# A two-stage conv block with a selective scan: C times B in wide GpSimd products ahead of the decays

## What is computed

```
x = x + _L0_conv_ref(_gn(x), ...)    # 8 experts: one scale for each image and channel
x = x + _L1_conv_ref(_gn(x), ...)    # selective scan, below

# _L1_conv_ref, N = 1024 tokens, 2 heads of 128 channels, S = 8 states
xz = silu(in_proj_w @ x + in_proj_b);  x_ssm, res, gate = split(xz, 3)
xf = silu(depthwise_conv3(x_ssm, dw_w) + dw_b)      # along the tokens
dbc = dbc_w @ xf + dbc_b                            # for each head 1 + 2*S rows: dt, B, C
dt = softplus(dt);  A = -exp(A_log)
# tokens in the order perm[head] (argsort of a Mobius map of the grid)
h_t = exp(dt_t * A) * h_(t-1) + dt_t * B_t * x_t    # for each state
y_t = sum over states of C_t * h_t,  + D[head] * x_t
# back to the image's order
y = y * silu(gate) + res
out = silu(out_proj_w @ y + out_proj_b)
```

## Time and profile before

| | |
|---|---|
| median of 3 runs | 1252.72 us (1245.59 to 1258.89) |
| span of the profiled execution | 1174.1 us; the profile does not give that execution's time as a run |
| PE busy | 961.5 us, 82% of the span |
| DVE, ScalarE, GpSimd busy | 588.0, 579.1, 532.4 us |
| stretch 543 to 674 us (phase 3): PE, DVE, ScalarE, GpSimd busy | 116.2, 64.2, 66.9, 68.5 of 131 us |
| chain that ended last | PE 41%, DMA 21%, GpSimd 16%, issue 10%, DVE 5%, SP's queue 4%, ScalarE 3% |
| GpSimd's `weigh` (L413) | 256 instructions, 182.1 us |
| DVE's product, reduction, diagonal and `mblk` (L1038, L1040, L1043, L1049) | 16 each, 38.8 + 59.4 + 7.8 + 36.7 us |
| ScalarE's table loads for softplus (L532, L534) | 8 each, 1283 ns one |

### The profile page before, as it was taken

The page is one execution under the profiler, slowest core; times in us unless marked ns, Lnnn a source line. Parts: engine busy times, 40 slices in busy tenths (PEclk is TensorE's granted clock), DMA queues, the critical chain, the costliest instruction groups (busy, mean ns, idle before and its releaser), DMA issues.

```text
span 1174.1 us, 12950 instructions
## 1 busy us (share of the span) xinstructions
PE 961.5 (82%) x3988; PEld 597.9 (51%) x3988; DVE 588.0 (50%) x1104; ACT 579.1 (49%) x1078; POOL 532.4 (45%) x628
## 2 busy tenths in 40 slices
PE   1039666997899988998899779997999889978966
PEld 0035445664467445754476346744575357634643
DVE  5966136534572448444753348243853466345613
ACT  4824423345734564547444564456553754456341
POOL 0002527164555627371826545471936373644340
PEclk9558765798899998999899989998999899998987
DMA  8830290135912391247513491238313661348122
GB/s 331 331 120 1 81 157 1 36 119 155 216 36 93 101 226 71 72 133 183 140 37 121 144 213 48 78 101 192 121 63 122 179 162 37 119 152 148 37 94 86
DMA packets 112051, 142.54 MB, mean 121 GB/s; under 512 B 41705, under 2 KB 91122, under 8 KB 111986
## 3 DMA queue, kind: packets, MB, share of 16 engines
q1 hardware_dynamic: 99698, 105.91, 34.0%
q0 software_dynamic: 12288, 35.80, 9.4%
HBM read 88.07 MB, written 53.61 MB: 121 GB/s over the span
## 4 chain that ended last, share of the span: by engine, by line
PE 41%; DMA 21%; POOL 16%; issue 10%; DVE 5%; SPq 4%; ACT 3%; POOLq 0%; ACTq 0%; DVEq 0%
PE pj L1183 12%; POOL xt_scratch L389 10%; PE pj L1258 9%; PE pj L1256 8%; DMA xb<-in_x 7%; DMA cd_scratch<-xp 6%; POOL big L401 4%; SPq L302 4%; PE st L1230 3%; DMA xp<-xt_scratch 2%; DMA xt_scratch<-stage,idx 2%; PE tp L1241 2%; PE tp L1206 2%; DMA crow<-cd_scratch 2%; POOL big L413 2%
## 5 line engine op out<-in xcount | busy, mean ns | idle before, releaser
L1183 PE MATMUL pj<-xb,wsc 128*128 128x512 f32 x768 | 392.1, 658 | 39.0 <-DMA xb<-in_x 26.6
L413 POOL TENSOR_TENSOR big<-big,crow 128x128 f32<-128x128 f32 x256 | 182.1, 751 | 212.6 <-DMA crow<-cd_scratch 199.1
L1183 PEld LDWEIGHTS pj<-xb,wsc 128*128 128x128 f32 x768 | 155.0, 213 | 205.9 <-issue 197.7
L389 POOL DMA_INDIRECT xt_scratch<-stage,idx x128 | 139.6, 1091 | 83.0 <-DVE stage L941 46.4
L358 POOL TENSOR_SCALAR wsc<-inw,pcur 128x256 f32<-128x256 f32 x96 | 62.6, 669 | 239.1 <-PE pj L1183 150.7
L401 POOL DMA_INDIRECT big<-yt_scratch,idx x128 | 130.5, 1020 | 75.5 <-issue 37.7
L1258 PE MATMUL pj<-ch 64*128 64x128 f32 x512 | 129.2, 333 | 0.0
L1256 PE MATMUL pj<-xp,mblk 128*128 128x128 f32 x512 | 120.1, 318 | 4.2 <-ACT xs L519 4.2
L1304 PE MATMUL pj<-gt,outw 128*128 128x512 f32 x256 | 111.8, 594 | 0.1
L995 DVE TENSOR_TENSOR_SCAN hs<-big,st 128x64 f32<-128x64 f32 x256 | 49.0, 265 | 101.8 <-PE st L1230 101.8
L570 ACT COPY ch<-tp 128x256 f32<-128x256 f32 x128 | 45.4, 376 | 106.6 <-PE tp L1242 106.6
(11 more groups left out here) (192 smaller groups left out, 1348.7 us busy)
## 6 DMA issues: line engine op xcount, KB each, us to landing
xb<-in_x SPq DMA_DIRECT2D x32, 1024.0 KB, 7.4
xp<-xt_scratch SPq DMA_DIRECT2D x8, 2048.0 KB, 10.0
crow<-cd_scratch SPq DMA_DIRECT2D x128, 128.0 KB, 7.8
yt_scratch<-rs SPq DMA_DIRECT2D x16, 1024.0 KB, 4.4
out<-xb SPq DMA_DIRECT2D x16, 1024.0 KB, 10.2
xp<-xt_scratch SPq DMA_DIRECT2D x8, 272.0 KB, 3.5
xt_scratch<-stage,idx POOLq DMA_INDIRECT x128
big<-yt_scratch,idx POOLq DMA_INDIRECT x128, 2.7
```

The costliest lines, as they stand in the source:

```text
L389: pool.indirect_dma_start(out=xt_d.ap(), out_offset=bass.IndirectOffsetOnAxis(ap=idx[:, k:k + 1], axis=0), in_=v(stage, (nt * H + h) * ROW ...
L413: last = nc.gpsimd.tensor_tensor(v(big, W_OFF + (s * Q + b * NT) * L, (L, NT), (1, L)), v(big, s * EEW + SEG + b * NT * L, (L, NT), (1, L) ...
L1183: last = nc.tensor.matmul(o[:, :], v(wsc, (b * CT + ct) * 2 * C + slot * C + ot * P, (1, P)), x_view(par, b, ct, nt * HALF, HALF), start=( ...
```

## The change

- **Products.** `weigh(i, h)` on GpSimd becomes `products(i, h)`. In place of decays times C, in 16 instructions of 128 columns, it forms C times (dt * B), in two instructions of 1024 columns, one for each image, and then adds the diagonal D (`dskip`) to state 0's part, 256 columns. It waits for `crow`, for `bc_step` (dt * B) and for the area at `W_OFF` to be free, and no longer for the decays.
- **DVE.** `token_weights` multiplies this by the decays, in one product of 2048 columns, and sums the eight states by three additions of 1024, 512 and 256 columns. The strided reduction (L1040) and the diagonal (L1043) go. `mblk` is written in two instructions, one for each image, and PE's `result` waits for its own image's.
- **Decays.** `decays(i, 1)` waits for DVE's product (`m_step`), since that is now what reads head 0's decays.
- **Table.** ScalarE's `softplus` starts with the load of the one table set that has both exp and ln.
- **`dskip`**, D on the diagonal for each head, is made once by two small DVE instructions ahead of `take_params(0, 0)`.

```diff
--- before.py
+++ after.py
@@ -122,8 +122,10 @@
         prm = sb("prm", B * PRM_W)
         pcur = sb("pcur", 2 * NB * PRM_W)
         idx = sb("idx", H * NT, U32)
+        dskip = sb("dskip", H * L)
         W_OFF = S * EEW
         A_SUM, A_SQ = 400, 400 + B
+        DB, DBE, CS = 0, Q * S, 2 * Q * S
 
 
         INB, DWW, DWB, OUTB, DBCB, ANEG, DPAR, MOB = 0, 6, 12, 14, 16, 50, 66, 68
@@ -178,6 +180,7 @@
         sg_full = sem("sg_full")
         ee_ready = sem("ee_ready")
         w_ready = sem("w_ready")
+        w_step = sem("w_step")
         bc_step = sem("bc_step")
         bblk_ready = sem("bblk_ready")
         cblk_ready = sem("cblk_ready")
@@ -394,7 +397,7 @@
                 hold(y_stored[h], 16 * (i + 1))
                 if h == 0:
 
-                    hold(mblk_ready, H * (i + 1))
+                    hold(mblk_ready, H * NB * (i + 1))
                     hold(hs_ready, H * NB * S * (i + 1))
                 for nt in range(NT):
                     k = h * NT + nt
@@ -402,19 +405,24 @@
                         out=v(big, k * NB * P, (1, NB * P)), out_offset=None, in_=yt_d.ap()[0:(h + 1) * N],
                         in_offset=bass.IndirectOffsetOnAxis(ap=idx[:, k:k + 1], axis=0)).then_inc(y_gathered[h], 16)
 
-            def weigh(i, h):
-
-                hold(ee_ready, i * H + h + 1)
+            def products(i, h):
+
                 hold(crow_in[h], 16 * CPT * (i + 1))
 
-                hold(m_step, (i * H + h) * 3)
-                for s in range(S):
-                    for b in range(NB):
-                        last = nc.gpsimd.tensor_tensor(
-                            v(big, W_OFF + (s * Q + b * NT) * L, (L, NT), (1, L)),
-                            v(big, s * EEW + SEG + b * NT * L, (L, NT), (1, L)),
-                            v(crow, h * NT * L * S * NB + s * NB + b, (L * S * NB, NT), (S * NB, L)), ALU.mult)
-                last.then_inc(w_ready, 1)
+                hold(bc_step, (i * H + h) * 3 + 1)
+
+                hold(m_step, (i * H + h) * 4)
+                if h == 0:
+
+                    hold(y_full, i * Y_U)
+                for b in range(NB):
+                    nc.gpsimd.tensor_tensor(
+                        v(big, W_OFF + b * NT * L, (Q * L, S), (1, NT * L)),
+                        v(crow, h * NT * L * S * NB + b, (NB, S), (S * NB, NT * L)),
+                        v(bc8, DB + b * NT * S, (1, S), (S, NT), (0, L)), ALU.mult).then_inc(w_step, 1)
+                hold(w_step, (i * H + h + 1) * NB)
+                skip = v(big, W_OFF, (L, Q), (1, L))
+                nc.gpsimd.tensor_tensor(skip, skip, v(dskip, h * L, (0, Q), (1, L)), ALU.add).then_inc(w_ready, 1)
 
             def first_tap(i, b):
 
@@ -427,14 +435,14 @@
 
             def cycle(i, par, half):
                 more = not last_phase(i)
-                weigh(i, 0)
+                products(i, 0)
                 if more:
                     if not first(i):
                         hold(pcur_ready, i + 2)
                         weights_x(i + 1, 1 - par, 0)
                     weights_x(i + 1, 1 - par, 1)
                 weights_residual(i, par)
-                weigh(i, 1)
+                products(i, 1)
                 if more:
                     weights_gate(i + 1, 1 - par, 0)
                     weights_gate(i + 1, 1 - par, 1)
@@ -528,6 +536,7 @@
 
             def softplus(i):
 
+                nc.scalar.preload_act_table_set("natural_log_exp_and_others")
                 act.wait_ge(sp_v, i * 9 + 1)
                 nc.scalar.activation(v(dts, 32, (1, 32)), v(dts, 0, (1, 32)), ACT.Exp, scale=-1.0).then_inc(sp_a, 1)
                 act.wait_ge(sp_v, i * 9 + 2)
@@ -541,7 +550,7 @@
                     wait(act, y_full, i * Y_U)
                 else:
 
-                    act.wait_ge(w_ready, i * H + h)
+                    act.wait_ge(m_step, (i * H + h - 1) * 4 + 1)
                     act.wait_ge(hs_ready, (i * H + h) * NB * S)
                 for s in range(S):
                     last = nc.scalar.activation(v(big, s * EEW, (1, EEW)), v(sg, 0, (1, EEW)), ACT.Exp,
@@ -942,7 +951,6 @@
 
             HQ = H * Q
             AXO, UO, WO, LO, MO, DO = 0, 32, 64, 96, 128, 192
-            DB, DBE, CS = 0, Q * S, 2 * Q * S
 
             def part(h, off):
                 return h * NT * ROW + NB * P + off
@@ -1034,20 +1042,23 @@
 
                 ih = i * H + h
                 dve.wait_ge(w_ready, ih + 1)
-                W = v(big, W_OFF, (Q * L, S), (L, Q), (1, L))
-                nc.vector.tensor_tensor(W, W, v(bc8, DB, (1, S), (S, Q), (0, L)), ALU.mult).then_inc(m_step, 1)
-                dve.wait_ge(m_step, ih * 3 + 1)
-                nc.vector.tensor_reduce(m16[:, :], v(big, W_OFF, (1, Q * L), (Q * L, S)), AX.X, ALU.add).then_inc(m_step, 1)
-                dve.wait_ge(m_step, ih * 3 + 2)
-
-                nc.vector.scalar_tensor_tensor(v(m16, 0, (L, Q), (1, L)), const("diag", (0, Q), (1, L)),
-                                               v(small, DPAR + h, (1, 1)), v(m16, 0, (L, Q), (1, L)),
-                                               ALU.mult, ALU.add).then_inc(m_step, 1)
-                dve.wait_ge(m_step, ih * 3 + 3)
+                dve.wait_ge(ee_ready, ih + 1)
+                states = lambda s0, n: v(big, W_OFF + s0 * Q * L, (Q * L, n), (1, Q * L))
+                nc.vector.tensor_tensor(states(0, S), v(big, SEG, (EEW, S), (1, Q * L)), states(0, S), ALU.mult).then_inc(m_step, 1)
+                dve.wait_ge(m_step, ih * 4 + 1)
+                nc.vector.tensor_tensor(states(0, 4), states(0, 4), states(4, 4), ALU.add).then_inc(m_step, 1)
+                dve.wait_ge(m_step, ih * 4 + 2)
+                nc.vector.tensor_tensor(states(0, 2), states(0, 2), states(2, 2), ALU.add).then_inc(m_step, 1)
+                dve.wait_ge(m_step, ih * 4 + 3)
+                nc.vector.tensor_tensor(m16[:, :], v(big, W_OFF, (1, Q * L)), v(big, W_OFF + Q * L, (1, Q * L)),
+                                        ALU.add).then_inc(m_step, 1)
+                dve.wait_ge(m_step, ih * 4 + 4)
 
                 wait(dve, ch_used, ih * 8)
-                nc.vector.tensor_tensor(v(mblk, 0, (P, Q), (L, CPT), (1, L)), v(m16, 0, (L, Q), (0, CPT), (1, L)),
-                                        const("causal", (0, Q), (L, CPT), (1, L)), ALU.mult).then_inc(mblk_ready, 1)
+                for b in range(NB):
+                    nc.vector.tensor_tensor(v(mblk, b * NT * P, (P, NT), (L, CPT), (1, L)),
+                                            v(m16, b * NT * L, (L, NT), (0, CPT), (1, L)),
+                                            const("causal", (0, NT), (L, CPT), (1, L)), ALU.mult).then_inc(mblk_ready, 1)
 
             def gated(i, h, b):
 
@@ -1103,6 +1114,8 @@
                     softplus(i + 1)
                 output(i, par, 1)
 
+            for h in range(H):
+                nc.vector.tensor_scalar(v(dskip, h * L, (1, L)), const("diag"), v(small, DPAR + h, (1, 1)), None, ALU.mult)
             take_params(0, 0)
             convolve(0, 0)
             for tile in tiles:
@@ -1248,7 +1261,7 @@
 
                 if gp == 0:
                     pj_slot(2 * b + 1, None, None, before)
-                    pe.wait_ge(mblk_ready, i * H + h + 1)
+                    pe.wait_ge(mblk_ready, (i * H + h) * NB + b + 1)
                 pe.wait_ge(t_drained, i * T_U + u + 1)
                 for e in range(2):
                     g = 2 * gp + e
```

## The result

The changed kernel takes 1269.02 us (1263.87 to 1271.44), beside 1255.33 us (1245.59 to 1258.89) for the kernel before: a ratio of 1.012, 95% interval 1.007 to 1.017. It is slower by 1.2%, where "no change" was forecast; the time lies 7 us above the range. The profiled execution has a span of 1264.9 us and was a run of 1266.7 us.

The account below looks back on a forecast made before the run. The prediction took the x load, behind other transfers on SP's queue, to bound the inner phases. Phase 0 -1.9, phase 7 -1.9, `dskip` +0.4 and phase 5 +1.0 gave -2.4 us on 1252.7: 1250, range 1238 to 1262.

Parts of the forecast that it names:

- 78.6 us lie outside the span, which I leave as they are.: Whole run: profiled span 1174.1 us against median 1252.7; the difference was taken as lying outside the span and unchanged.
- The first rival: PE in inner phases: x load lands before PE asks, so the table load's saving comes through, -8 us, 1241; chance 0.17.
- The slack of the inner phases: Phases 1 to 6: the x load holds PE, leaving gate evictions behind head 1's decays 0 to 4.1 us of slack.
- This wait does not move: D = 0.: ScalarE's decays of head 1: waiting for DVE's product, 7.6 to 7.7 us after `crow`, adds no delay D over 7.7 before.
- P = 4.9 us: GpSimd, head 0: two wide products of 2.0 us, the add 0.7 and a wait 0.2, in place of 7.69 us.
- DVE's part: DVE, per head: product 2.3 us, additions 2.33, `mblk` halves about 1.2 each; reduction and diagonal, 4.2, become 2.3.
- That is hidden: Head 1: DVE's factors could stand 4 us behind both wide products, covered by DVE ending head 0's weights some 4 us sooner.
- Phase 0, -1.9 us: Phase 0: PE's first result starts at 184.8 instead of 186.68, then held by ScalarE's gate evictions; -1.9 us.
- Phase 7, -1.9 us: Phase 7: scaled weights come 2.8 us sooner, but PE's third unit then waits for gate eviction 6; gain -1.9 us.
- The table set, worth nothing: ScalarE's softplus: `rtot` comes 1.15 us sooner, but PE waits 1.15 us longer for x in phases 1 to 6.
- The +1.0 us for phase 5: Phase 5: a longer PE idle of 3.85 us ahead of slower matmuls costs 0 to 2.0 us, taken as +1.0.
- The slower rival: GpSimd's wide products take 3.84 us each, D = +3.7 us, PE waits for gate evictions; +15 us, 1268; chance 0.13.

Follow-up runs that it names:

- e2: The changed kernel as it stands, measured again on chip 0, against the kernel before: ratio 0.9995 [0.996, 1.003].
- e1: The kernel before, unchanged, measured again on chip 0 (before 1182.5 us): ratio 1.0009 [0.997, 1.005].
- e16: Kernel before with only ScalarE's decays of head 1 waiting for DVE's product of head 0, chip 5 (before 1264.7 us): ratio 1.0113 [1.009, 1.014].
- e3: Kernel before with only the table set load added to softplus, chip 0 (before 1182.5 us): ratio 1.0006 [0.997, 1.004].
- e9: Kernel before with only the table set load added to softplus, repeated on chip 2 (before 1249.2 us): ratio 1.0017 [0.999, 1.004].
- e11: Changed kernel with `mblk` written in one instruction again, chip 2, against the kernel before (1249.2 us): ratio 1.0157 [1.012, 1.020].
- e5: Changed kernel with the three additions put back to the single reduction, chip 2, against the kernel before (1252.4 us): ratio 1.0135 [1.010, 1.017].
- e7: Changed kernel with GpSimd's residual weights ahead of head 0's products, chip 2, against the kernel before (1252.4 us): ratio 1.0156 [1.012, 1.019].
- e10: Changed kernel without the table set load, chip 2, against the kernel before (1249.2 us): ratio 1.0124 [1.008, 1.017].

## Why the prediction was wrong, step by step

- **"78.6 us lie outside the span, which I leave as they are."** Wrong, and the root of the miss. They lie inside, in stalls of the way back and of the loop boundaries. A span 6% short of the median was the one sign, ahead of time, that trace and runs were not of the same kind; I turned it into a constant. The first rival, built on "transfers run more freely", had the right condition (x no longer waited for) but put a gain on it.
- **The slack of the inner phases**, 0 to 4.1 us, from the x wait. Nothing on the 1180 chips speaks against it. On the others the x waits are 0 in phases 3 and 5 and 0.3 to 2.9 us elsewhere.
- **"This wait does not move: D = 0."** This is the step that failed within the kernel. I compared P + product with `weigh`, both counted from `crow`'s landing, and left out what stands ahead of the product on DVE, the second scan. Where `crow` lands late (1180 chips) the scan is long past: 8.28 us from `crow` to ScalarE in phase 7 of e2 against 7.73 in e1, D = 0.55, near enough. Where it lands early, the old wait was covered by the scan and the new one is scan plus product: D = 1.44 us visible, and in phase 3 3.0 with the clock. e16 shows that this wait is enough for a loss of this size, with the reserve on its other phases named there; that it is also needed for it, no run shows.
- **P = 4.9 us.** Mis-sized: 4.97 + 0.18 + 0.72 = 5.87 us in e2. A wide product takes 2.49 us and not 2.0, 2.4 ns an element; the fixed part of the single-input rows did not carry over. The estimate by the Trainium skill, GPSIMD Engine Reference, section 3.1 (4497 ns for a two-input instruction of 2048 elements, some 2.2 ns each), was 5.3 us for P and nearer. By D this cost half a microsecond on 1180 chips.
- **DVE's part**: product 2.28, additions 1.24 + 0.71 + 0.49 = 2.44 (2.33 forecast), `mblk` halves 1.26 each: right.
- **"That is hidden"**, of the wide products' lock: in head 1 yes. DVE's two instructions of L1022 run from 181.98 to 187.06 in phase 0 after, and the two wide products of head 1 from 181.85 to 186.93. This agrees with the exclusive lock that the Trainium skill, SBUF — State Buffer, section Who interferes with whom, describes. But I looked for it in head 1 only. In phases 3 and 5 of a 1250 chip it also falls on head 0, ahead of `bblk`, where PE waits.
- **Phase 0, -1.9 us**: right on both. PE idled 2.16 us ahead of its first result in place of 4.21 (e2 against e1), and phase 0 is 2.6 us shorter in the table above, 1.8 of it up to the first result.
- **Phase 7, -1.9 us**: wrong. On the 1180 chips PE starts 11.45 us behind `crow` instead of 11.56: the additions, unlike the reduction, slow GpSimd's weights (5.53 us for four instead of 3.88) and eat what the products saved. On the others the decays hold it, and it is 6.1 us longer: 3.8 in `project` and 3.4 in head 1 at the lower clock, less 1.8 before `project`.
- **The table set, worth nothing; `dskip`, +0.4**: right (e3, e9; two of 0.23 us). The +1.0 us for phase 5 is not tested: two traces of the kernel before already differ there, with an x wait of 2.69 us and of 4.53 us (e1).
- **The slower rival** named the right wait and the right place to look (PE waiting for gate evictions), but for another reason, products of 3.84 us; the products did not decide.

Of the 13.5 us in the table of phases 7.7 can be assigned: `project` and the start of phase 3 (3.1 + 0.3) and of phase 5 (1.5 + 1.6), `project` in phase 7 (3.8), less phase 0 (2.6). Two more items are found but not explained: 2.7 us in the way back of phase 5, whose stalls differ by up to 3 us from phase to phase of one kernel, and the 3.4 us of head 1 in phase 7 at the lower clock shown above, which e11 has too and e5, e7 and e10 do not. The other phases differ by small amounts both ways. Open too: the share of the wide products' hold on DVE (seen in the trace, isolated by no run on a 1250 chip).

## What to carry to other kernels

Ahead of everything else compare the profiled execution's span with the timed runs; if they differ by more than the runs do among themselves, every slack read from that trace is of another situation, and a forecast needs both. When a wait is moved to another engine's instruction, count it from what is queued ahead of that instruction, not only from its inputs, and do so for inputs that come early as well as late. A wait of PE that grows from 0.8 to 2.2 us cost 1.4 us in half of the cases here and 3.1 us in the other half, by the clock behind it.
